# An eight-core attention and FFN layer: waits taken out of the first projection, and a cast moved from VectorE to ScalarE

## What is computed

```python
q1, k1, q2, k2, v = (heads(x @ w.T) for w in (q1_w, k1_w, q2_w, k2_w, v_w))
attn1 = softmax(q1 @ k1.T / sqrt(128)); attn2 = softmax(q2 @ k2.T / sqrt(128))
out = (attn1 - lam * attn2) @ v            # per head, then heads side by side
x = layernorm(x + out @ o_w.T)
absmax = max(abs(x), axis=-1); scale = maximum(absmax, 1e-7) / 127
q = clip(round(x / scale), -128, 127)      # int8
ffn = (q @ weight.T) * scale * w_scale + bias   # float16
x = layernorm(x + ffn)
```

## Time and profile before

| | |
|---|---|
| median of 2 runs | 3210.63 us |
| the profiled execution | 3212.7 us, span 3211.2 us on core 3 |
| spans of the eight cores | 3204.4 to 3211.2 us |
| TensorE busy | 2954.5 us, 92% of the span |
| VectorE busy | 1289.3 us, 40% |
| ScalarE busy | 1271.5 us, 40% |
| mean granted TensorE clock | 0.984 on core 3, 0.984 to 0.986 on all |

### The profile page before, as it was taken

The page is one execution under the profiler, slowest core; times in us unless marked ns, Lnnn a source line. Parts: engine busy times, 40 slices in busy tenths (PEclk is TensorE's granted clock), DMA queues, the critical chain, the costliest instruction groups (busy, mean ns, idle before and its releaser), DMA issues.

```text
span 3211.2 us, 45249 instructions; the slowest of 8 cores (3204.4 to 3211.2 us)
## 1 busy us (share of the span) xinstructions
PE 2954.5 (92%) x16640; PEld 1455.2 (45%) x16640; DVE 1289.3 (40%) x1585; ACT 1271.5 (40%) x1347; POOL 44.7 (1%) x85
## 2 busy tenths in 40 slices
PE   1999999999999999999999999999999998886997
PEld 0545454545454545454545454545454543333443
DVE  0122424242424242424343333343434247676576
ACT  0071717171707171717171717171717172332222
POOL 0000000000000000000000000000000000000000
PEclk9999999999999999999999999999999999888998
DMA  9665202020202020101011111111000132435233
GB/s 157 144 171 155 38 2 38 3 39 2 40 1 40 5 36 7 34 10 32 13 28 16 25 19 22 21 20 24 17 3 6 48 105 80 122 110 189 96 115 118
DMA packets 93427, 172.79 MB, mean 54 GB/s; under 512 B 68160, under 2 KB 68160, under 8 KB 86688
## 3 DMA queue, kind: packets, MB, share of 16 engines
q0 software_dynamic: 14016, 86.38, 14.0%
q1 hardware_dynamic: 79200, 83.51, 8.1%
HBM read 174.07 MB, written 50.33 MB: 70 GB/s over the span
## 4 chain that ended last, share of the span: by engine, by line
PE 87%; DVE 5%; DMA 3%; ACT 2%; issue 2%; another core or an unknown queue 0%; DVEq 0%; ACTq 0%; SPq 0%; POOL 0%; POOLq 0%
PE psA L240 14%; PE psB L240 14%; PE psA L257 7%; PE psB L257 7%; PE pO L276 6%; PE pS L279 6%; PE pS L278 6%; PE pO L277 6%; PE psA L224 4%; PE psB L224 4%; PE pffnA L709 3%; PE pffnB L709 3%; ACT pb L306 2%; PE pattnL L503 2%; DMA xTb<-xT 1%
## 5 line engine op out<-in xcount | busy, mean ns | idle before, releaser
L306 ACT ACTIVATE pb<-psA 128x1024 bf16<-128x1024 f32 x512 | 525.1, 1026 | 1151.4 <-PE psA L257 1151.4
L306 ACT ACTIVATE pb<-psB 128x1024 bf16<-128x1024 f32 x512 | 525.2, 1026 | 121.8 <-PE psB L257 121.8
L240 PE MATMUL psA<-xTb,wq 128*128 128x512 bf16 x2048 | 464.6, 380 | 0.3 <-issue 0.3
L240 PE MATMUL psB<-xTb,wq 128*128 128x512 bf16 x2048 | 462.9, 379 | 0.0
L43 DVE RECIPROCAL r<-sc_ 128x512 f32<-128x512 f32 x128 | 429.2, 3353 | 13.9 <-DVE r L43 0.5
L43 DVE COPY sc_<-pS 128x512 f32<-128x512 f32 x128 | 88.5, 692 | 772.5 <-PE pS L284 765.9
L257 PE MATMUL psA<-q,k 128*128 128x512 bf16 x1024 | 304.4, 379 | 81.4 <-ACT pb L306 80.8
L279 PE MATMUL pS<-pb,ones 128*128 128x512 bf16 x960 | 363.8, 379 | 0.0
L278 PE MATMUL pS<-pb,ones 128*128 128x512 bf16 x960 | 363.8, 379 | 0.0
L277 PE MATMUL pO<-pb,v 128*128 128x512 bf16 x960 | 363.8, 379 | 0.0
L276 PE MATMUL pO<-pb,vv 128*128 128x512 bf16 x960 | 363.7, 379 | 0.0
(11 more groups left out here) (96 smaller groups left out, 2119.0 us busy)
## 6 DMA issues: line engine op xcount, KB each, us to landing
wq<-wqkv POOLq DMA_DIRECT2D x15, 2560.0 KB, 19.3
xin<-x SPq DMA_DIRECT2D x16, 1024.0 KB, 8.1
out<-oo SPq DMA_DIRECT2D x16, 1024.0 KB, 4.7
xTb<-xT POOLq DMA_DIRECT2D x4, 2048.0 KB, 39.6
stg<-wo POOLq DMA_DIRECT2D x16, 512.0 KB, 6.2
wob<-stg SPq DMA_DIRECT2D x16, 512.0 KB, 2.7
stg<-wffn POOLq DMA_DIRECT2D x16, 512.0 KB, 4.8
wfb<-stg SPq DMA_DIRECT2D x16, 512.0 KB, 2.9
```

Source lines behind the costliest of these rows:

```text
L240: mm = te.matmul(projb[g % 2][:, 0:512], wslice(m + 1, c), xT_sb[:, c * S + qt * 512: c * S + qt * 512 + 512], start=(c == 0), stop=(c == ...
L306: sc.activation(pb_sb[:, (s % 3) * 1024:(s % 3) * 1024 + 1024], sbank[c % 2][:], AF.Exp, scale=INV_SQRT_HD,).then_inc(sEXP, 1)
```

## The change

Three edits at the start and one in o-proj.

- POOL issues the load of the second quarter of x before its wait for the first part of wq, and so before the rest of wq. The other loads keep their order.
- TensorE waits once for all four quarters of x before its first matmul, and for all of head 0's wq (sWQ at 32) at the top of head 0. The waits inside head 0's V loop and those before its q projection are gone.
- In o-proj, the cast of q8 to `qb_sb` goes from VectorE to ScalarE. VectorE's q8 now signals sAF2, and waits, for k >= 1, until the previous cast is done (sQ). ScalarE casts tile tt - 1 between its sum of squares of tile tt and `evacs(tt - 2)`, behind waits for sAF2 and for the transposes of the tile before; the last cast stands between the last square root and the last four evacuations.

```diff
                 g.dma_start(out=wq_sb[:, 0:4096], in_=wqkv_d[0, :, 0:4096]).then_inc(sWQ, 16)
                 g.dma_start(out=xtv[:, 0:4, :], in_=xdv[:, 0:4, :]).then_inc(sXT, 16)
+                g.dma_start(out=xtv[:, 4:8, :], in_=xdv[:, 4:8, :]).then_inc(sXT2, 16)
                 g.wait_ge(sWQ, 16)
                 g.dma_start(out=wq_sb[:, 4096:10240], in_=wqkv_d[0, :, 4096:10240]).then_inc(sWQ, 16)
-                g.dma_start(out=xtv[:, 4:8, :], in_=xdv[:, 4:8, :]).then_inc(sXT2, 16)
                 g.dma_start(out=xtv[:, 8:12, :], in_=xdv[:, 8:12, :]).then_inc(sXT3, 16)
...
             def _(te):
+                for _s in (sXT, sXT2, sXT3, sXT4):
+                    te.wait_ge(_s, 16)
                 for h in range(H):
-                    te.wait_ge(sWQ, 16 if h == 0 else 16 * (h + 2))
+                    te.wait_ge(sWQ, 16 * (h + 2))
...
                         for c in range(NC_):
-                            if h == 0:
-                                te.wait_ge((sXT, sXT2, sXT3, sXT4)[c // 4], 16)
...
-                    if h == 0:
-                        te.wait_ge(sWQ, 32)
-                        for _s in (sXT2, sXT3, sXT4):
-                            te.wait_ge(_s, 16)
...
                                       AF.Square, accum_out=st2_sb[:, tt % 2:tt % 2 + 1]).then_inc(sST, 1)
+                        if tt >= 1:
+                            sc.wait_ge(sAF2, tt)
+                            if tt >= 2:
+                                sc.wait_ge(sTR, 2 * (tt - 1))
+                            sc.copy(qb_sb[:], q8_sb[:]).then_inc(sQ, 1)
                         if tt >= 2:
                             evacs(tt - 2)
                     sc.wait_ge(sVST, NT)
                     sc.activation(st5_sb[:], st6_sb[:], AF.Sqrt).then_inc(sSQT, 1)
+                    sc.wait_ge(sAF2, NT)
+                    sc.wait_ge(sTR, 2 * (NT - 1))
+                    sc.copy(qb_sb[:], q8_sb[:]).then_inc(sQ, 1)
                     evacs(NT - 2)
                     evacs(NT - 1)
...
                         ve.tensor_scalar(t_sb[:], y_sb[:], st6_sb[:], MAGIC, OP.mult, OP.add)
-                        ve.tensor_scalar(q8_sb[:], t_sb[:], MAGIC, None, OP.subtract)
                         if k >= 1:
-                            ve.wait_ge(sTR, 2 * k)
-                        ve.tensor_copy(qb_sb[:], q8_sb[:], inc=(sQ, 1, k + 1))
+                            ve.wait_ge(sQ, k)
+                        ve.tensor_scalar(q8_sb[:], t_sb[:], MAGIC, None, OP.subtract,
+                                         inc=(sAF2, 1, k + 1))
```

## The result

| | before | after |
|---|---|---|
| median | 3211.21 us (8 executions, 3210.42 to 3212.34) | 3184.59 us (9 executions, eight of them 3182.08 to 3187.63) |
| ratio | | 0.9917, interval 0.9906 to 0.9928 |
| the profiled execution | 3212.7 us, span 3211.2 us on core 3 | 3184.05 us, span 3182.5 us on core 4 |
| TensorE's share of the chain | 87% | 86% |

The change takes 26.6 us off, 0.8%; the forecast was 3181, with a range of 3168 to 3190. Some executions had one half of the chip (cores 0 to 3 or 4 to 7) at a lower clock; the ratios and the medians of the experiments leave them out, and "n executions" there counts the others.

The account below looks back on a forecast made before the run. TensorE was taken as the bound (87% of the chain), with losses at the start, in o-proj and at its end. Terms -17.9 - 1.5 - 9.3 + 1.5 - 2.3 = -29.5 took 3212.7 to 3183.2, less 2.1 to 3181 us; range 3168 to 3190.

Parts of the forecast that it names:

- The pace of head 0: Head 0's V groups: long-fulfilled waits before every matmul set 2.23 us a group; without them V ends 17.9 us earlier.
- Rival (b): Head 0's V: running DMAs or something else, not the waits, set the pace, so V stays at 2.23; 3202 us, chance 0.06.
- Rival (c): Head 0's V: weight loads set the pace once the waits are gone, 9.2 us more; 3190 us, chance 0.06.
- The start's size: Start, head 0: V ends 17.9 us earlier and the first Q group gains a net 1.5 us.
- the other 222 at 0.0567: Head 0's V: after 34 matmuls at low clock, 222 run at head 2's 0.0567 us each, 12.6 us.
- The turn: O-proj, two-tile period: one of two casts lies on it, 1.33 us over seven turns, -9.3 us; period 36.2 us.
- Rival (d): O-proj: the cast isn't on the turn, ScalarE or the ocol load takes the 1.33 us back; 3190 us, chance 0.08.
- The clock term: O-proj, seven gaps: one fall of the granted clock avoided at 2.3 us each, -2.3 us; bounds 0 and 7 falls.
- Rival (a): O-proj gaps: the clock stays up in six instead of one, 11.5 us more gained; 3169.5 us, chance 0.12.
- The tail: End of o-proj: the longer last cast, ahead of tile 14's evacuations, delays the FFN's start by 1.5 us.
- Rival (e): O-proj: ScalarE becomes the turn once its cast exceeds 5.2 us; slower than before, 3222 us at 10 us; chance 0.02.
- The sum: Whole kernel: all terms together -29.5 us, 3212.7 to 3183.2 for the profiled execution, forecast 3181 after taking off 2.1.

## Why the prediction was right, step by step

**The pace of head 0 was right.** The waits before each matmul, not the clock and not the DMA, set 2.23 us a group; put back alone they cost 19 us by the medians, and 35.3 us in place of 19.8 for V on the slowest cores. Rival (b) fell with that run. Rival (c), weight loads, fell with the groups 0.89 us apart. So did the figure of the Trainium skill, page TensorE: Matmul & The Clock Gate, section Back-to-back issue gap: 81 ns for each pair of a weight load and a 128-column matmul, where the changed kernel's groups give 0.893 / 16 = 56 ns.

**The start's size was 3 us too large.** The step that failed is "the other 222 at 0.0567": it took the pace of head 2 and left out that in head 0 a 2560 KB load runs beside it. Forecast -17.9 - 1.5 = -19.4, measured -16.4. V took 19.8 us (72.69 to 92.5) in place of 16.2. Against the forecast went the standstill (88.21 - 84.81 - 0.89 = 2.5) and the fall of the clock behind it (the two groups that followed took 3.4 us in place of 1.8, so 1.6 more). For it, the slow stretch at V's beginning was 0.5 shorter, V began 0.4 earlier, and the first Q group won 0.2 more than I had booked. The fall was the very loss that I had booked as removed with the first Q group. Without the loads beside it, the same 256 matmuls took 15.6 to 16.9 us on the eight cores (89.43 - 72.58 = 16.85 on core 2), where the prediction had 16.2. No kernel has the reordered load of x by itself, so how much of the 0.4 it made isn't shown.

One reading of the prediction is weaker than it sounds. The end of that slow stretch, at about 76.7 before and 75.4 after, follows from the matmuls' durations (266 and then 216 ns; 314 and then 219 ns). The granted clock in the windows is 1.00 there all the time, from 73.0 and from 72.5 on.

**The turn was right, and its size.** 36.2 us forecast, 35.8 measured; the earlier trace rows named the cast that lies on it, and the two kernels with half of the casts each show that it is this one and no other. Rival (d) fell with them. Of the 14.2 us of the seven turns the cast makes the 9.3 that were forecast, and the half tiles behind the gaps 1.5 (next paragraph). Another 2.8 the prediction did not have: the loads of ocol, from issue to landing, took 7.33 us in place of 8.89 at the first turn, and 32.6 in place of 33.8 at the six others together. Why they were shorter isn't shown; 0.6 is left.

**The clock term was right in size for another reason.** I took one fall avoided of seven, 2.3 us. On core 4 none is avoided. But four of the seven were cheaper. In the gap of the earlier trace rows the clock was low from 2769.7 to 2776.5, and the half tile behind it took 9.39. In the changed kernel the gaps that end at 2749.18, 2820.43 and 2891.37 show falls at 2748.3, 2820.0 and 2891.7, so 0.5 and 0.1 us before the restart and 0.5 behind it, low stretches of only 3.4 us, and half tiles of 8.12, 8.33 and 8.54 (without their first record); at tile 3 the low stretch was 6.8 us, where it was 10.2 before. The last of them in windows (length, busy PE, clock, DMA share, GB/s):

```profile
2890.00:2891.00 1.00, 0.00 (x0) 1.00 1.16 320
2891.00:2892.00 1.00, 0.63 (x3) 0.84 1.09 451
...
2894.00:2895.00 1.00, 1.00 (x4) 0.50 0.00 0
2895.00:2896.00 1.00, 1.00 (x6) 0.96 0.00 0
```

From their restart to the next half tile, with the missing first matmul, the seven half tiles behind the gaps take 63.0 us, those of before 65.2: 2.3 less in all, 1.5 of it in the turns and 0.8 behind the last restart. That it is the 2.3 of the forecast is luck. The gaps ahead of the other three are hardly longer (3.89, 3.66 and 3.04 us in the rows, the cheaper ones 3.66, 3.19 and 2.85), and their half tiles took 9.4 to 9.9, as before; why the two kinds alternate isn't shown. Rival (a), a clock that stays up, needed the gap away altogether; the later write of y did that, and only there its mechanism is seen.

**The tail was right.** +1.5 forecast. On the six cores with complete records the second half of tile 15 starts 35.6 us ahead of the FFN before and 37.2 after: +1.6. The +1.9 of the table is 1.9 of this on core 4 against core 3, less 0.8 for the half tile at the restart, and 0.8 more in the FFN. The casts in their order, core 4:

```profile
2932.30 1.90 ACT L555 CAST qbf<-qi 128x2048 bf16<-128x2048 int8 x1 [9.15 <-DVE qi L43]
...
2935.00 1.02 ACT L525 COPY qT<-ptrB 128x1024 bf16<-128x1024 bf16 x1
```

The cast ahead of the evacuations is what costs; the kernel with the other order won 1.9 back. Rival (e) was far from deciding. Its threshold fits the kernel with three casts, but its formula left out two things: a longer cast counts twice at the tail, and the clock gives back what the turns lose.

**The sum.** By the profiled executions the forecast was -29.5 and the result -28.7: the start short by 3.0, the turns over by 2.6 (14.2 for 9.3 + 2.3; 1.6 of it at the first turn, 2.9 instead of 1.33, by its shorter load), and what lies behind them 0.4 longer. So part of the agreement is a sum of misses. The rest of the distance between 3181 and 3184.6 is mostly my step from one execution to the median: I took the 2.1 us by which the profiled execution of before was over its median off the forecast too, but the profiled execution after lay 0.5 under its own.

## What to carry to other kernels

Look at the pace of a stretch beside the same instructions elsewhere in the same trace: the same 16 groups at 2.23 us in head 0 and at 0.91 in head 2 gave away that waits long fulfilled were the price, and one wait ahead of the loop does for all of them. Before a step is moved off an engine, follow one whole turn from the restart back to itself and count which of its instances lies on it: here one cast in two did, and the other half of the move only made the tail longer. And when the turn ends with a load, ask first what stands ahead of it in its queue: a few lines of order brought 39 us where the moved cast brought 9.

## What the runs showed of the hardware

- With a semaphore wait, fulfilled long before, ahead of each 128-column matmul, TensorE takes 138 ns a matmul, at a granted clock of 0.50 and of 0.86 alike. Without the waits it takes 56 ns at 1.00, so a wait costs 82 ns there; at 0.50, against 106 ns, some 32.
- A dense stretch of weight loads and 128-column matmuls stood still for 0.97 to 2.61 us with a large load beside it, on all eight cores of the changed kernel, and on none with the load held back. In the other kernels with this start it is 0.3 to 2.9 us, and missing on single cores. The clock can fall behind such a standstill (cores 0 and 4).
- The clock behind a gap of TensorE comes back after different times: low from 2769.7 to 2776.5 in the kernel before, from 2891.7 to 2895.1 in the changed one. The half tile behind the gap took 8.7 to 9.9 us with the longer low stretch and 8.3 to 8.6 with the shorter one, in place of 6.9. In the changed kernel, whose gaps are about 2.5 us shorter, core 4 shows the shorter stretch at three of seven; the kernel before shows none on core 3.
